# GpSimd's four dispatch transfers per token tile: one step later, spread between its other operations

## The reference

```python
x = x + attention(layernorm(x))          # 16 heads of 8, RoPE, causal, window of 64 keys
x = x + ffn(layernorm(x))
# ffn: a shared expert, and 32 experts of hidden size 256
shared = silu(xf @ sg) * (xf @ su) @ sd
# routing: 4 of 8 groups by score, then the 4 best experts of those groups, gates = softmax
pos = cumsum(onehot(expert))[...] - 1     # place of a token in its expert's list
keep = pos < capacity                     # capacity 640 for each expert
buf[expert, pos] = xf[token]              # dispatch: a scatter of rows
h = silu(buf @ wg) * (buf @ wu); out_e = h @ wd
routed[token] += gate * out_e[expert, pos]
```

## Time and profile before

| | |
|---|---|
| timed runs, median of 3 | 726.87 us (725.57 to 731.16) |
| span of the profiled execution | 904.6 us |
| the profiled execution against the median | span 177.7 us longer |
| PE busy | 724.0 us, 80% |
| DVE busy | 534.0 us, 59% |
| POOL busy | 415.1 us, 46% |
| ACT busy | 360.9 us, 40% |
| mean granted TensorE clock | 0.829 |

### The profile page before, as it was taken

How to read it: one execution, slowest core, us unless ns; L and a number is a source line. 1 busy time by engine, 2 the same in 40 slices (tenths; PEclk the granted TensorE clock), 3 DMA queues, 4 the chain that set the end, 5 groups by cost and what they waited for, 6 DMA issues and landing times.

```text
span 904.6 us, 24570 instructions
## 1 busy us (share of the span) xinstructions
PE 724.0 (80%) x7521; PEld 563.5 (62%) x7521; DVE 534.0 (59%) x2192; ACT 360.9 (40%) x853; POOL 415.1 (46%) x548
## 2 busy tenths in 40 slices
PE   3798888988978788898888858888888888877960
PEld 1565656665646565575665637777777777777540
DVE  3476756556577676656666656545454454543598
ACT  4465544454455445444454423332323232322200
POOL 4125343353343434334344350555555555556555
PEclk9698776676798878767788859999999999998985
DMA  8991000000000000000000002423233333421355
GB/s 268 358 390 35 14 20 15 12 23 12 12 22 10 20 9 15 10 7 14 6 7 6 6 8 84 125 76 105 76 114 107 114 115 103 126 75 32 122 182 167
DMA packets 52338, 68.37 MB, mean 76 GB/s; under 512 B 9505, under 2 KB 31807, under 8 KB 52304
## 3 DMA queue, kind: packets, MB, share of 16 engines
q1 hardware_dynamic: 38240, 53.56, 18.4%
q0 software_dynamic: 9216, 11.97, 4.4%
q10 hardware_dynamic: 4848, 2.40, 0.9%
HBM read 34.89 MB, written 39.99 MB: 83 GB/s over the span
## 4 chain that ended last, share of the span: by engine, by line
PE 52%; another core or an unknown queue 19%; issue 10%; DVE 10%; ACT 6%; POOL 1%; ACTq 1%; DVEq 1%; POOLq 0%
PE bank L693 9%; PE bank L864 7%; PE bank L680 6%; PE bank L674 5%; PE bank L663 5%; PE bank L657 3%; PE bank L701 3%; DVE x_all L1246 3%; DVE mx L1044 2%; PE bank L733 2%; ACT hact L607 2%; PE bank L817 2%; PE bank L756 1%; PE bank L747 1%
## 5 line engine op out<-in xcount | busy, mean ns | idle before, releaser
L463 POOL DMA_INDIRECT pair_results<-yout,yidx x160 | 157.2, 982 | 143.4 <-ACT yout L625 104.0
L447 POOL DMA_INDIRECT expert_slots<-xfe,sidx x128 | 127.0, 992 | 141.5 <-DVE sidx L1148 108.3
L864 PE MATMUL bank<-xgT_parts,wgu_parts 128*128 128x320 f32 x768 | 147.2, 344 | 46.4 <-ACT hact L607 46.4
L864 PEld LDWEIGHTS bank<-xgT_parts,wgu_parts 128*128 128x128 f32 x768 | 125.9, 208 | 57.3 <-ACT hact L607 50.3
L519 ACT ACTIVATE pt<-bank 128x512 f32<-128x512 f32 x128 | 76.2, 596 | 182.2 <-PE bank L680 164.9
L1259 DVE TENSOR_TENSOR hact<-hact,bank 128x320 f32<-128x320 f32 x128 | 57.1, 481 | 140.2 <-ACT hact L607 133.1
L1044 DVE TENSOR_REDUCE mx<-bank 128x4 f32<-128x512 f32 x128 | 87.3, 683 | 32.5 <-PE bank L663 19.7
L421 POOL TENSOR_TENSOR pout<-pin,mhalf 128x3 f32<-128x3 f32 (+2 forms) x36 | 29.9, 830 | 127.4 <-DVE pin L970 127.4
L890 PE MATMUL bank<-wdn,hact 128*128 128x128 f32 x640 | 82.7, 288 | 2.3 <-issue 2.3
L890 PEld LDWEIGHTS bank<-wdn,hact 128*128 128x128 f32 x640 | 82.5, 207 | 2.5 <-issue 2.5
L623 ACT COPY yout<-bank 128x512 f32<-128x512 f32 x32 | 18.7, 585 | 162.2 <-remote 151.0
(11 more groups left out here) (148 smaller groups left out, 1335.1 us busy)
## 6 DMA issues: line engine op xcount, KB each, us to landing
expert_slots<-fill SPq DMA_DIRECT2D x32, 322.5 KB, 6.5
xg<-expert_slots SPq DMA_DIRECT2D x32, 322.5 KB
pair_results<-rload SPq DMA_DIRECT2D x32, 256.0 KB
rload<-pair_results SPq DMA_DIRECT2D x16, 512.0 KB, 4.0
wgu<-in_L_ffn_wg_dram SPq DMA_DIRECT2D x32, 128.0 KB
wgu<-in_L_ffn_wu_dram SPq DMA_DIRECT2D x32, 128.0 KB
wdn<-in_L_ffn_wd_dram SPq DMA_DIRECT2D x32, 128.0 KB
pair_results<-yout,yidx POOLq DMA_INDIRECT x160
```

Source lines behind the costliest of these rows:

```text
L447: g.indirect_dma_start(out=slots_d, out_offset=bass.IndirectOffsetOnAxis(ap=sidx[:, tr.b, k:k + 1], axis=0), in_=xfe[:, tr.b, k, :], in_of ...
L463: g.indirect_dma_start(out=pairs_d, out_offset=bass.IndirectOffsetOnAxis(ap=yidx[:, c, j:j + 1], axis=0), in_=yout[:, c, j, :], in_offset= ...
L864: last = mm(bank[2 + 2 * w + h][:, 0:CH], wgu_parts[:, e.b, wp, w, h * P:(h + 1) * P], xgT_parts[:, e.b, xp, ch * CH:(ch + 1) * CH], start ...
```

## The change

Three things change together.

1. A seventh tile, `td` = tau-5, is handed to every `step`. GpSimd's transfers are for `td` and no longer for `tr`: they go one step later.
2. They no longer stand four in a row at the end of the step. Transfer 0 is the step's first operation and holds the waits; transfer 1 follows `rr`, transfer 2 follows the power, transfer 3 follows the two subtractions.
3. A row buffer is now in use for longer, so `xfe` has four buffers and `dispatched` four semaphores (`NX = 4`). The loop's body must then be four steps: steps -1 to 7 are written out, 8 to 27 are a loop of 5 turns with four steps each, and 28 to 36 are written out. `sidx` keeps two buffers, and VectorE's wait before it is now for the transfers of tile `tr`-2.

```diff
+NX = 4
+Turn = namedtuple("Turn", "n half b lap x")
+def turn_of(lap, x):
+    return Turn(NX * lap + x, 2 * lap + x // 2, x % 2, lap, x)
...
-        xfe = sb("xfe", [P, 2, TOPK, ROW])
+        xfe = sb("xfe", [P, NX, TOPK, ROW])
...
-            FIRST = 6
-            LAST = FIRST + (NT - 1 - FIRST) // 2 * 2
+            FIRST = 8
+            LAST = FIRST + (NT - 1 - FIRST) // NX * NX
...
-            with eng.Fori(0, (LAST - FIRST) // 2) as i:
-                for c in range(2):
+            with eng.Fori(0, (LAST - FIRST) // NX) as i:
+                for c in range(NX):
...
-            for tau in range(LAST, NT + 4):
+            for tau in range(LAST, NT + 5):
...
-            def step(tau, tn, tf, tp, ts, tw, tr):
+            def step(tau, tn, tf, tp, ts, tw, tr, td):
+                def dispatch(k):
+                    if td is None:
+                        return
+                    if k == 0:
+                        if isinstance(td.n, int) and td.n == 0:
+                            pool.wait_ge(S.filled, 16 * NE)
+                        pool.wait_ge(S.slot_ready, td.n + 1)
+                        pool.wait_ge(S.xfe_id, td.n + 1)
+                        pool.wait_ge(S.xf_ready, td.n + 1)
+                        pool.wait_ge(S.xf_copied, td.n + 1)
+                        hold(pool)
+                    g.indirect_dma_start(
+                        out=slots_d, out_offset=bass.IndirectOffsetOnAxis(ap=sidx[:, td.b, k:k + 1], axis=0),
+                        in_=xfe[:, td.x, k, :], in_offset=None, bounds_check=NSLOT - 1,
+                        oob_is_err=False).then_inc(dispatched[td.x], 16)
+                dispatch(0)
...
                     g.tensor_tensor(rr[:, b], ra[:, :], rb[:, :], ALU.add).then_inc(S.rope_r, 1)
+                dispatch(1)
...
+                dispatch(2)
...
+                dispatch(3)
...
-                    for k in range(TOPK):
-                        g.indirect_dma_start(
-                            out=slots_d, out_offset=bass.IndirectOffsetOnAxis(ap=sidx[:, tr.b, k:k + 1], axis=0),
...
                 def slots_c():
                     dve.wait_ge(S.slots, 4 * tr.n + 4)
-                    wait(dve, dispatched[tr.b], 16 * TOPK * tr.half)
+                    sent = turn_of(tr.lap + (tr.x - 2) // NX, (tr.x - 2) % NX)
+                    wait(dve, dispatched[sent.x], 16 * TOPK * (sent.lap + 1))
```

More of the change, by code:

```diff
@@ L233, in block_kernel @@
         S = namedtuple("Semaphores", names)(*[sem(n) for n in names])
-        dispatched = [sem(f"dispatched{b}") for b in range(2)]
+        dispatched = [sem(f"dispatched{x}") for x in range(NX)]
         wgu_arrived = [sem(f"wgu_arrived{b}") for b in range(2)]
@@ L327, in _ @@
                 load_wdn(e, e)
-            for b in range(2):
-                sp.wait_ge(dispatched[b], 16 * TOPK * (NT // 2))
+            for x in range(NX):
+                sp.wait_ge(dispatched[x], 16 * TOPK * (NT // NX))
             for e in range(2):
@@ L430, in step @@
                      .then_inc(S.split_lo, 1)
+                dispatch(3)
                 if tw is not None:
-                    wait(pool, dispatched[tw.b], 16 * TOPK * tw.half)
+                    wait(pool, dispatched[tw.x], 16 * TOPK * tw.lap)
                     hold(pool)
-                    g.tensor_copy(xfe[:, tw.b, :, D:ROW], pair[:, bass.ds(tw.n, 1), :].rearrange("p o k -> p k o"))\
+                    g.tensor_copy(xfe[:, tw.x, :, D:ROW], pair[:, bass.ds(tw.n, 1), :].rearrange("p o k -> p k o"))\
                      .then_inc(S.xfe_id, 1)
[L437 to L445, removed]
-                    for k in range(TOPK):
-                        g.indirect_dma_start(
-                            out=slots_d, out_offset=bass.IndirectOffsetOnAxis(ap=sidx[:, tr.b, k:k + 1], axis=0),
-                            in_=xfe[:, tr.b, k, :], in_offset=None, bounds_check=NSLOT - 1,
-                            oob_is_err=False).then_inc(dispatched[tr.b], 16)
             attention_steps(pool, step)
@@ L540, in step @@
                     act.wait_ge(S.xf_ready, tr.n + 1)
-                    a.copy(xfe[:, tr.b, 1:TOPK, 0:D], xfe[:, tr.b, 0:1, 0:D].broadcast_to([P, TOPK - 1, D]))\
+                    a.copy(xfe[:, tr.x, 1:TOPK, 0:D], xfe[:, tr.x, 0:1, 0:D].broadcast_to([P, TOPK - 1, D]))\
                      .then_inc(S.xf_copied, 1)
@@ L973, in second_norm @@
                     dve.wait_ge(S.pow_done, tau + 2)
-                    wait(dve, dispatched[tw.b], 16 * TOPK * tw.half)
+                    wait(dve, dispatched[tw.x], 16 * TOPK * tw.lap)
                     wait(dve, S.xfT_done, tw.n - 1)
-                    v.tensor_scalar(xfe[:, tw.b, 0, 0:D], row(tw),
+                    v.tensor_scalar(xfe[:, tw.x, 0, 0:D], row(tw),
                                     mv2[:, tw.b, 0:1], pout[:, tw.b, 1:2], ALU.subtract, ALU.mult)\
```

12 lines of the change are left out of this document (6 added, 6 removed).

## The result

The changed kernel takes 743.01 us (median of 4 runs, 739.53 to 744.95) against 726.22 us (4 runs, 724.31 to 731.16) beside it: a ratio of 1.0217, 95% interval 1.0158 to 1.0276. It is slower by 2%, and outside the forecast range of 699 to 742 us. Two later comparisons of the same two kernels gave 740.70 against 726.88 us (1.0199, 1.0147 to 1.0251) and 736.20 against 726.62 us (1.0119, 1.0068 to 1.0170). Medians here are of all runs shown, while the ratios leave out every run that lies more than 1.5% above the fastest of the same kernel.

The account below looks back on a forecast made before the run. No engine was full; attention steps were bound by a chain mostly through PE, the burst's circle just covered. The sum was 27 x 0.0 less 2 us for the loop: 726.87 - 2, rounded to 725 us; range 699 to 742 us.

Parts of the forecast that it names:

- The reading of the hold: Unnamed waits, 174.6 us of the first profile's chain, were taken as nearly absent from timed runs: 904.6 - 174.6 = 730.0 us.
- the hold: Attention and expert stages, first profile: during POOL's transfer bursts, what PE finished is not seen; 2.56 us in the step shown.
- The hold rival: The hold is in timed runs too, so spreading the transfers gives back at least 21 us: 706 us; chance 0.12.
- The step without the hold: One attention step less its 2.56 us unnamed wait: 14.63 - 2.56 = 12.07 us, 11.50 in the middle case.
- "issue" time: Attention chain: 9.4%, 1.13 us of 12.07, stepping between recorded instructions; half, 0.57, taken off for timed runs.
- Nothing per step: Attention step, middle case: 11.81 us after the change against 11.79 before, so no gain or loss.
- The burst's circle: Attention step, L1148 through transfers, `rr`, casts and back: 11.99 us, just covered; as rival bounding timed steps, 709 us, chance 0.22.
- The third transfer: Between power and subtractions: costs 1.27 us, making PE 0.18 late, 0.31 taken; as deciding rival, 740 us, chance 0.14.
- the cover: Attention step: 1.11 us between the subtractions' end and PE's transposes, set against the third transfer's 1.27 us.
- The loop: Attention loop, 5 turns for 12: seven branches fewer gain 1 us, five more written-out steps another 1 us.
- The first hint, four times a fetch: Rival: DVE or PE refetches the loop's head at four back-branches, 3 to 28 us, 10 taken: 735 us; chance 0.10.

Follow-up runs that it names:

- the fifth experiment: The changed kernel itself, unmodified, run again as base for the runs that vary whose attention steps are looped: 740.70 us (4 runs), ratio 1.0199 to the kernel before.
- the loop of four alone: Kernel before with the loop of four steps and four row buffers, transfers left together at their own step's end: 734.26 us (10 runs), later 734.58 us (12 runs).
- experiment 9: Kernel before with only DVE's attention loop taking four tiles a turn instead of two, buffers and transfers untouched: 735.96 us (5 runs), ratio 1.0160.
- experiment 8: Changed kernel with DVE's loop beginning at step 16 instead of 8, so two branches back instead of four: 737.65 us (4 runs), ratio 1.0144.

## Why the prediction failed

*The reading of the hold: right.* It took 174.6 us off the first trace and foresaw a kernel that has no hold in timed runs. The span was predicted to fall by much more than the median; it fell by 167 us (904.6 to 737.6), where 20 to 60 were forecast, because a second execution has no hold, change or not. The hold rival is refuted.

*The step without the hold: 0.2 us too short.* 11.79 us were worked out for the kernel before and 11.81 for the changed one, both with their loops. With its loop the kernel before measures 11.98 us in an execution of 727.16 us, so the half of the "issue" time that was taken off is there in a run at the median. That the kernel before written out measures 11.82 (11.824 and 11.815) is luck: the prediction had no loop cost in its step. Written out the changed kernel has 11.99. "Nothing per step" was off by 0.15 us, 4 us in all, of which the medians show 0 to 1.

*The burst's circle: right that it bounds nothing.* ACT does wait for `rr` in 29 of 32 steps before, more than the first trace showed, and still the steps keep their length when it doesn't: another chain, through PE's L693, L680 and L674, is as long. The 11.99 against 12.07 us of the prediction said so.

*The third transfer: right mechanism, right size.* 0.18 us of lateness for PE was worked out from the rows (and 0.31 taken, for a shorter step); 0.18 is what the rows above show. As a rival at 740 us, with 0.5 us a step, it is refuted, for the cover holds.

*The loop: wrong, and it decided.* This is the step that failed. The term counted seven branches fewer as 1 us of gain, and five steps more written out as another; measured, the changed kernel loses 14.9 us by DVE's loop. It should have counted how long the body of a turn is on each engine. The first hint, four times a fetch, stood as a rival at 735 us with a chance of 0.10 and a place named ("an idle DVE or PE of over 1 us once every four steps"). That is what happened; its range of 3 to 28 us holds the 14.9 us measured for DVE's loop, but the 10 us taken were too low, because the clock's falls behind the stops were not in it. Its price was read from q8, whose packets have 16 KB; the packets in DVE's stops are those of q14, with 8 KB. The prediction set against it that DVE idles there anyway; that slack took 1 of the 3 us. It had no row that counts a body's instructions, and 0.10 was far too little for a rival against which no row spoke.

The sum as it should have stood, in the changed kernel's own profile: four stops of 2.7 to 3.0 us, of which 2.0 us each reach the step (8.1 us), one fall of the clock (2.7 us), the rest 1.4 us, together 12.2 us on 725.4. Other executions have more falls: the profile of the fifth experiment has three, and 14.7, 13.8 and 15.8 us in the steps that follow three of the four long ones.

The Trainium skill ("Runtime: NRT & Kernel Launch", "Instruction fetch mechanics") states that a taken branch to a target outside a window of two pages of 256 instructions stalls until it is fetched. The trace agrees in kind: a body of 212 records has no stop on DVE, one of 413 has one at every branch back (2.6 to 3.1 us) with a packet of instructions in it, though 413 is less than 512. By the Trainium skill's figures (an estimate) a body of 413 touches three pages unless it begins within the first 99 instructions of one, and one of 212 never more than two; where in a page a body begins no row here shows.

*Still open.* Why the clock falls behind some stops and not behind others; what the other engines' loops cost exactly (about 3 us in the changed kernel, 4 to 6 us for all loops of the kernel before); and whether the delayed transfers cost 0 or 5 us in the loop (the fourteen runs have a mean of 739.3 us, the twenty-two of the loop of four alone 733.9, but beside each other 2).

A version that beats both exists: either kernel with its attention steps written out, 720.6 to 722.7 us, 0.4 to 0.8% below the kernel before.

## What to carry to other kernels

Before a loop's turn is made longer, count the instructions of its body on every engine, not the branches saved: here 212 records stayed on DVE and 413 cost it a stop of 3 us at each branch back, and the time lost was 2.6 us a branch (10.3 us for four, experiment 9) to twice the stop (experiment 8). In a profile look for "issue" pieces of 2 to 3 us in the chain at equal distances, and then for a packet of an instruction queue inside one of them. Where a profiled execution is a quarter longer than the median, take another before costing any wait in it.

## What the runs showed of the hardware

- DVE's stop at a branch back: 2.6 to 3.1 us in every kernel with the body of four tiles in a loop, always ahead of the turn's first instruction, in the loop that begins at step 16 with a second one of 1.2 us behind each. In the changed kernel each stop has one packet of 8 KB of q14 in it, and each full turn five. GpSimd (107 records a turn), ScalarE (167) and TensorE (833) showed none of over 1.1 us there.
- The instructions of q14 come in packets of 8 KB (0.34 MB in 41), of q8 in 16 KB (0.44 MB in 27).
- TensorE's granted clock from 60 to 380 us: 1.00 in all seven profiles in which DVE has no such stop, 0.91 to 0.98 in all ten in which it has (the first profile of the kernel before, with the hold, is in neither).
- Single executions can be far longer than all others: the first profile of the kernel before has a span of 904.6 us, and one run of the changed kernel written out took 1090.83 us, at a mean granted clock of 1.0, where the eleven others took 720.89 to 724.56 us. There is no trace of the second, so whether it had the same hold is not shown.
